# The first unit of a selective-scan block prepared by rows of its own

## The chip, the cores and the metric

The kernel runs on one core of a Trainium2 chip. The metric is the device time of one execution in microseconds. Five engines work side by side, each through its own list of instructions in order, and wait for one another by semaphores: TensorE (PE; matmuls into PSUM), VectorE (DVE), ScalarE (ACT), GpSimd (POOL), and SyncE (SP), whose queue issues DMA transfers. ScalarE can issue DMA transfers too. In the profile PEld is TensorE's load of weights, and SPq the issuing of DMAs on SyncE's queue.

## The reference, cut to what matters

x is 4 x 1024 x 128. A state-space block, a layer norm, a feed-forward block with weights and activations rounded to FP4 in blocks of 16, and another layer norm:

```python
u = silu(xp[:, :-2] * conv_w[0] + xp[:, 1:-1] * conv_w[1] + xp[:, 2:] * conv_w[2])
B, C = split(u @ W_bc + b_bc)                       # 16 states each
A = -exp(A_log)
dt = softplus((u @ W_dt + b_dt) @ W_dtp + b_dtp)
h[l] = exp(A * dt[l]) * h[l-1] + B[l] * x[l] * dt[l]   # per channel and state
y[l] = sum over the states of C[l] * h[l]
x = layernorm(x + y + x * Dcoeff)
hidden = silu(fp4(x) @ fp4(w_gate).T) * (fp4(x) @ fp4(w_up).T)
x = layernorm(x + fp4(hidden) @ fp4(w_down).T)
```

## The kernel before

The 4096 positions are cut into eight units of 512 (`UNITS`); two units make one sequence. Channels lie on the partitions. For the scan the 128 channels are cut into four quarters (`QUADS`) of 32, and each tile of 128 partitions holds 4 states x 32 channels, so there are 4 sets of states (`SETS`) x 4 quarters = 16 groups (`GROUPS`) in a unit.

The work is a pipeline in software. `run` calls on each engine `step(a, s, f, g, h, p)`: `s` is the unit that is scanned, `a` the next one, which is prepared meanwhile, and `f`, `g`, `h` are the three before, in the stages of the feed-forward block. Inside a step the engine goes through 16 slots k, one for each group; the table `AT` says in which slot a stage's instructions stand. The order of each engine's list is thus written by hand. The first call, with i = -1, has no `s`: it only prepares unit 0 (slot 0 transposes, slots 1 and 2 convolution, and so on) and does what the weights need before the first scan (`setup`, `setup_weights`).

The preparation of a unit, engine by engine:
- TensorE turns x (`ps_prep<-ident,x_tok`), ScalarE copies it to `x_feat`; TensorE convolves with three diagonal matrices (`tap_diag`, six matmul passes) and ScalarE takes tanh; VectorE makes `u_feat` (half of silu's argument times 1 + tanh).
- TensorE multiplies u by `wz` (W_dt W_dtp, itself made at the start), and ScalarE makes dt by Softplus, once into `dtx` and once into PSUM. Exp and tanh share a table of ScalarE, Softplus needs another, hence table loads around it. VectorE writes dt * x as the second half of `dtx`.
- SyncE's queue copies `dtx` to `dt_rep`, each of 4 quarters to 4 blocks of 32 partitions: 16 DMAs of 128 KB (`replicate`), counted per quarter by `dt_in`.
- TensorE makes C for each set (`ps_prep<-u_feat,wbc_rep`), four times two passes in the one bank `ps_prep`, and ScalarE takes each out to `c_rep`.

The scan of a unit: TensorE makes B for a set in `ps_b` (`spread_b`); VectorE multiplies it with the four quarters of `dt_rep` at once (`times_b`, the "product with B", 128x2048, into `db`); ScalarE makes the decays by Exp, one for each group (`decay`, `ps_decay`), two groups ahead; VectorE scans (`scan`, 16 for a unit, one for each group); GpSimd multiplies the states by C (`times_c`, two groups at a time); TensorE sums over the states in `ps_y` (`sum_states`). `times_b` for set m + 1 stands two groups ahead of its first scan, so the first one of the next unit comes before scan 14 of this one.

The feed-forward weights are rounded to FP4 by nine operations on VectorE (`quant_op` 0 to 8, into `qh_amax`, `qh_scale`, `qh_inv`, `qh_norm`, `qh_magic`, `hq`), turned by TensorE and taken by ScalarE to `gate_t`, `up_t` and `down_t`.

## Time and profile before

| | |
|---|---|
| time, median of 3 runs | 410.14 us (409.21 to 410.53) |
| the profiled execution's own time | 411.21 us |
| its span in the trace | 409.4 us |
| mean granted TensorE clock | 0.859 of full speed |
| busy: PE, DVE, ACT, POOL | 284.3 (69%), 333.6 (81%), 216.1 (53%), 281.5 (69%) us |
| DMA | 21.86 MB in 19246 packets, mean 53 GB/s |

Times in a view count from the span's start. A row of a timeline gives start, duration, engine, line, operation, output<-inputs, shapes, how many were merged, and in brackets the idle time before and what ended it. The granted clock is the share of TensorE's full 2.4 GHz that it was allowed; it has two levels, 0.5 and 1, and a number between is a mean over the stretch.

### The profile page before, as it was taken

How to read it: one execution, taken by the hardware profiler on the slowest of the kernel's cores; microseconds unless marked ns; L12 is line 12 of the kernel's file. 1: busy time of each engine (PE TensorE's matmuls, PEld its weight loads, DVE VectorE, ACT ScalarE, POOL GpSimd, SP SyncE). 2: the span in 40 equal slices, each digit the busy share in tenths (PEclk: the TensorE clock that was granted, in tenths of full speed). 3: DMA queues.
4: the chain of work that ended last, by engine and by line, in shares of the span. 5: the costliest groups of instructions: out<-in, count | busy, mean ns of one | idle time of the engine just before them, and what ended most of it. 6: DMA issues, size and time to landing. Idle time of an engine off the chain costs nothing.

```text
span 409.4 us, 3984 instructions
## 1 busy us (share of the span) xinstructions
PE 284.3 (69%) x1136; PEld 133.2 (33%) x1136; DVE 333.6 (81%) x374; ACT 216.1 (53%) x493; POOL 281.5 (69%) x168
## 2 busy tenths in 40 slices
PE   5478665677866784789397848778578765664783
PEld 2125111212412333334242325233333342234363
DVE  2828969799999999699978999699969998445880
ACT  2634663765575566465927482756546364133235
POOL 0003555568487997499929994799749995976652
PEclk9656698889969996999889996999699668598698
DMA  2470280081018005410261008100530000000001
GB/s 39 109 169 0 52 181 1 0 186 44 2 44 189 0 2 114 92 51 2 51 155 52 0 2 189 48 19 2 126 80 27 0 0 26 1 2 1 26 2 51
DMA packets 19246, 21.86 MB, mean 53 GB/s; under 512 B 6096, under 2 KB 15128, under 8 KB 19224
## 3 DMA queue, kind: packets, MB, share of 16 engines
q1 hardware_dynamic: 19224, 21.60, 23.2%
q8 instruction: 9, 0.15, 0.2%
q14 instruction: 13, 0.11, 0.1%
HBM read 2.72 MB, written 2.10 MB: 12 GB/s over the span
## 4 chain that ended last, share of the span: by engine, by line
PE 31%; POOL 27%; ACT 13%; issue 11%; DVE 11%; SPq 4%; DMA 2%; POOLq 0%; DVEq 0%; ACTq 0%
POOL product L654 8%; PE ps_f L1151 5%; PE ps_b L1111 5%; POOL qh_norm L675 4%; POOL qh_norm L670 4%; DVE states L862 4%; PE ps_prep L1089 4%; PE ps_y L1069 3%; DVE db L849 3%; PE ps_prep L1104 3%; PE ps_f L1149 2%; SPq L412 2%; POOL rstd L664 2%; POOL xq L694 2%; POOL qx_norm L675 2%
## 5 line engine op out<-in xcount | busy, mean ns | idle before, releaser
L654 POOL TENSOR_TENSOR product<-states,c_rep 128x1024 f32<-128x1024 f32 x64 | 150.7, 2360 | 60.3 <-DVE states L862 57.1
L450 ACT ACTIVATE ps_decay<-dt_rep,aneg 128x512 f32<-128x512 f32 x128 | 87.0, 693 | 38.2 <-DVE states L862 38.1
L862 DVE TENSOR_TENSOR_SCAN states<-ps_decay,states,db 128x512 f32<-128x512 f32 x64 | 79.9, 1263 | 14.1 <-POOL product L654 9.5
L849 DVE SCALAR_TENSOR_TENSOR db<-ps_b,bbc_rep,dt_rep 128x2048 f32<-128x2048 f32 x32 | 74.8, 2338 | 11.7 <-PE ps_b L1111 9.4
L862 DVE TENSOR_TENSOR_SCAN states<-ps_decay,db 128x512 f32<-128x512 f32 x64 | 76.3, 1207 | 8.6 <-issue 4.6
L1104 PE MATMUL ps_prep<-u_feat,wbc_rep 128*128 128x512 f32 x64 | 39.5, 701 | 22.5 <-ACT c_rep L516 19.4
L1111 PE MATMUL ps_b<-u_feat,wbc_rep 128*128 128x512 f32 x64 | 43.3, 765 | 16.4 <-DVE db L849 16.4
L1069 PE MATMUL ps_y<-product,gather 128*32 128x512 f32 x256 | 39.1, 687 | 6.0 <-POOL product L654 5.7
L1136 PE MATMUL ps_f<-gate_t,xq_t 128*128 128x352 f32 x64 | 30.1, 554 | 14.5 <-DVE hidden L916 8.9
L516 ACT ACTIVATE c_rep<-ps_prep,bbc_rep 128x512 f32<-128x512 f32 x32 | 22.1, 692 | 28.2 <-PE ps_prep L1104 28.2
L662 POOL TENSOR_TENSOR var_eps<-var,eps 128x4 f32<-128x4 f32 x16 | 3.5, 220 | 45.8 <-ACT hq_t L524 39.3
L554 ACT ACTIVATE gate_tanh<-ps_f 128x352 f32<-128x352 f32 x32 | 14.8, 464 | 36.8 <-PE ps_f L1136 36.8
L1089 PE MATMUL ps_prep<-x_feat,tap_diag 128*128 128x512 f32 x48 | 28.3, 711 | 5.4 <-ACT x_feat L491 4.6
L1149 PE MATMUL ps_f<-x,ident 128*128 128x128 f32 x44 | 12.3, 371 | 23.2 <-ACT hq_t L562 23.2
L1104 PEld LDWEIGHTS ps_prep<-u_feat,wbc_rep 128*128 128x128 f32 x64 | 10.4, 205 | 50.7 <-ACT c_rep L516 41.5
L524 ACT ACTIVATE hq_t<-ps_f 128x128 f32<-128x128 f32 x22 | 5.8, 278 | 39.9 <-PE ps_f L1151 39.9
L1144 PE MATMUL ps_f<-up_t,xq_t 128*128 128x352 f32 x64 | 26.3, 495 | 0.7 <-ACT y_out L575 0.7
L1111 PEld LDWEIGHTS ps_b<-u_feat,wbc_rep 128*128 128x128 f32 x64 | 13.8, 236 | 32.1 <-DVE db L849 21.4
L1151 PE MATMUL ps_f<-down_t,hq_t 128*128 128x128 f32 (+1 forms) x120 | 23.2, 348 | 0.0
L916 DVE SCALAR_TENSOR_TENSOR hidden<-gate_tanh,ps_f 128x352 f32<-128x352 f32 x32 | 16.1, 502 | 8.1 <-ACT gate_tanh L554 7.9
L1151 PEld LDWEIGHTS ps_f<-down_t,hq_t 128*128 128x128 f32 (+1 forms) x120 | 21.5, 262 | 0.0
L1136 PEld LDWEIGHTS ps_f<-gate_t,xq_t 128*128 128x128 f32 x64 | 10.4, 203 | 32.2 <-DVE hidden L916 21.9
(150 smaller groups left out, 505.1 us busy)
## 6 DMA issues: line engine op xcount, KB each, us to landing
dt_rep<-dtx SPq DMA_DIRECT2D x128, 128.0 KB, 2.4
x_tok<-in_L_attn_x SPq DMA_DIRECT2D x8, 256.0 KB, 3.0
out<-y_out SPq DMA_DIRECT2D x8, 256.0 KB, 2.3
hidden<-in_L_ffn_w_down SPq DMA_DIRECT2D x1, 176.0 KB, 2.5
x_feat<-in_L_attn_x SPq DMA_DIRECT2D x8, 0.5 KB, 2.7
hidden<-in_L_ffn_w_gate SPq DMA_DIRECT2D x1, 128.0 KB, 2.2
hidden<-in_L_ffn_w_up SPq DMA_DIRECT2D x1, 128.0 KB, 2.2
alog<-in_L_attn_A_log SPq DMA_DIRECT2D x4, 8.0 KB
```

Of the source, the lines that this page charges most:

```text
L450: nc.scalar.activation(ps_decay[BANK_OF[k]][:], dt_rep[p][:, c, 0, :], ACT.Exp, scale=aneg[:, c, m:m + 1]).then_inc(decay_done, 1)
L654: nc.gpsimd.tensor_tensor(product[:, j % PRODUCTS], states[p][:, first:first + 2, :], over(c_rep[p][:, j // SET_PAIRS, :], 2), ALU.mult).t ...
L675: order.mark(nc.gpsimd.tensor_tensor(b.norm[:, 0:width], b.norm[:, 0:width], b.magic[:, 0:width], ALU.subtract))
L849: nc.vector.scalar_tensor_tensor(out=db[m % DB][:], in0=over(ps_b[:], QUADS), scalar=bbc_rep[:, 0, m:m + 1], in1=dt_rep[p][:, :, 1, :], op ...
L862: nc.vector.tensor_tensor_scan(out=states[p][:, k % ring, :], data0=ps_decay[BANK_OF[k]][:], data1=db[k // QUADS % DB][:, k % QUADS, :], i ...
L1069: last = nc.tensor.matmul(ps_y[c * E:(c + 1) * E, :], gather[:], product[:, (m * SET_PAIRS + c // 2) % PRODUCTS, c % 2, :], start=False, s ...
L1089: last = nc.tensor.matmul(ps_prep[:], tap_diag[:, tap], x_feat[o][:, tap:tap + UNIT], start=(tap == 0), stop=(tap == 2))
L1104: nc.tensor.matmul(ps_prep[:], wbc_rep[:, 1, m], u_feat[o][:], start=True, stop=True)\
L1111: nc.tensor.matmul(ps_b[:], wbc_rep[:, 0, m], u_feat[o][:], start=True, stop=True).then_inc(b_mm, 1)
L1136: nc.tensor.matmul(ps_f1[:, 0:INNER], xq_t[:, i * 128:(i + 1) * 128], gate_t[:], start=True, stop=True).then_inc(gate_mm, 1)
L1144: nc.tensor.matmul(ps_f2[:, 0:INNER], xq_t[:, i * 128:(i + 1) * 128], up_t[:], start=True, stop=True).then_inc(up_mm, 1)
L1151: last = nc.tensor.matmul(bank[:, columns], hq_chunk(j, rows), down_t[0:rows, j, :], start=False, stop=(j == 2))
```

## The change

Unit 0 is no longer prepared by a call of `step`; each engine has a `head` of its own, and `run` starts with i = 0.

- **Convolution of unit 0 on VectorE**: three operations over 512 columns from `x_feat` with `half_taps`, into `conv_0` (room in `product`). `tap_diag` is made later, for unit 1 on. `wz` and `bz` are taken out by VectorE instead of ScalarE.
- **dt of unit 0** is made once, and VectorE makes dt * x from the copy in SBUF.
- **Copies from two queues**: SyncE copies quarters 0, 2 and 3 of unit 0, ScalarE's queue quarter 1; the four DMAs of `A_log` are issued by ScalarE at its very start instead of by SyncE.
- **C of unit 0 in `ps_y`**: `c_of_first` makes C for the first set in the head, and for the others in slots 0, 1 and 2 of the first step; the sums of that step wait until all are out (`head_c_done`).
- **First product with B in two halves** of two quarters (`half_times_b`); the second stands before scan 2. The second product with B of unit 0 moves to slot 4, and its matmul to slot 3 of TensorE.
- **Weights**: the last three operations of the FP4 rounding move to GpSimd; VectorE does the first six in the head. Turning them moves from slots 1 and 3 of the first step to 6 and 9, and taking them out from 2 and 4 to 7 and 10.

```diff
-    for i in range(-1, UNITS):
+    for i in range(UNITS):
...
+            replicate(Unit(0), 0, (0, 2, 3))
...
+            channels = a_log.rearrange("(c a e) k -> c a e k", c=QUADS, a=1)
+            for c in range(QUADS):
+                act.dma_start(alog[:, c, :], channels[c].broadcast_to([STATES, E, N])).then_inc(alog_in, 16)
...
+            def head(a):
+
+                act.wait_ge(prep_mm, 1)
+                nc.scalar.activation(x_feat[0][:, 1:UNIT + 1], ps_prep[:], ACT.Copy).then_inc(prep_evac, PREP_EVAC)
+                act.wait_ge(conv_done, 1)
+                nc.scalar.activation(tanh_c[:], conv_0, ACT.Tanh).then_inc(tanh_done, 1)
+                act.wait_ge(alog_in, 16 * QUADS)
+                nc.scalar.activation(aexp[:].rearrange("p c k -> p (c k)"), alog[:].rearrange("p c k -> p (c k)"),
+                                     ACT.Exp).then_inc(scan_ready, 1)
+                act.wait_ge(scan_ready, 1)
+                for n in range(STATES):
+                    rows = slice(n * E, (n + 1) * E)
+                    nc.scalar.activation(aneg[rows], aexp[rows].rearrange("p c (m n) -> p n c m", n=STATES)[:, n],
+                                         ACT.Copy, scale=-1.0).then_inc(scan_ready, 1)
+                act.wait_ge(z_ready, 2)
+                nc.scalar.activation(table_in[:, 1:2], bz[:], ACT.Softplus)
+                act.wait_ge(prep_mm, PREP_MM)
+                nc.scalar.activation(dtx[:, 0, :], ps_prep[:], ACT.Softplus, bias=bz[:]).then_inc(dt_out, 1)
+                act.wait_ge(dtx_done, 1)
+                act.wait_ge(dt_out, 1)
+                for n in range(STATES):
+                    act.dma_start(dt_rep[0][n * E:(n + 1) * E, 1], dtx[E:2 * E]).then_inc(dt_in[1], 16)
+                nc.scalar.activation(table_in[:, 2:3], bz[:], ACT.Exp)
+                act.wait_ge(scan_ready, 1 + STATES)
+                act.wait_ge(selectors, 1)
+                for k in range(AHEAD):
+                    decay(a, k, 0)
+                c_of_first(0)
+
+            def c_of_first(m):
+                act.wait_ge(head_c, m + 1)
+                nc.scalar.activation(c_rep[0][:, m, :], ps_y[:], ACT.Identity,
+                                     bias=bbc_rep[:, 1, m:m + 1]).then_inc(head_c_done, 1)
...
+                            if k < SETS - 1:
+                                c_of_first(k + 1)
...
-                if j == 0:
+                if j % SET_PAIRS == 0 and not s.beyond(1):
+                    pool.wait_ge(head_c_done, j // SET_PAIRS + 1)
...
+            nc.vector.tensor_scalar(half_taps[:], taps[:], 0.5, None, ALU.mult).then_inc(conv_order, 1)
...
+            dve.wait_ge(conv_order, 1)
+            dve.wait_ge(prep_evac, PREP_EVAC)
+            nc.vector.tensor_scalar(conv_0, x_feat[0][:, 1:UNIT + 1], half_taps[:, 1:2], None,
+                                    ALU.mult).then_inc(conv_order, 1)
+            dve.wait_ge(conv_order, 2)
+            nc.vector.scalar_tensor_tensor(out=conv_0, in0=x_feat[0][:, 0:UNIT], scalar=half_taps[:, 0:1], in1=conv_0,
+                                           op0=ALU.mult, op1=ALU.add).then_inc(conv_order, 1)
+            dve.wait_ge(conv_order, 3)
+            dve.wait_ge(halo_in[0], 16)
+            nc.vector.scalar_tensor_tensor(out=conv_0, in0=x_feat[0][:, 2:UNIT + 2], scalar=half_taps[:, 2:3], in1=conv_0,
+                                           op0=ALU.mult, op1=ALU.add).then_inc(conv_done, 1)
+            dve.wait_ge(z_weights, 1)
+            nc.vector.tensor_copy(wz[:], ps_f1[:, 0:D]).then_inc(z_ready, 1)
+            nc.vector.tensor_tensor(bz[:], ps_f1[:, D:D + 1], bdtp[:], ALU.add).then_inc(z_ready, 1)
+            dve.wait_ge(conv_done, 1)
+            dve.wait_ge(tanh_done, 1)
+            nc.vector.scalar_tensor_tensor(out=u_feat[0][:], in0=tanh_c[:], scalar=1.0, in1=conv_0,
+                                           op0=ALU.add, op1=ALU.mult).then_inc(u_done, 1)
...
+            def head():
+                dve.wait_ge(dt_out, 1)
+                nc.vector.tensor_tensor(dtx[:, 1, :], dtx[:, 0, :], x_feat[0][:, 1:UNIT + 1], ALU.mult).then_inc(dtx_done, 1)
+                for i in range(3):
+                    last = nc.vector.tensor_scalar(tap_diag[:, i], ident[:], half_taps[:, i:i + 1], None, ALU.mult)
+                setup.mark(last)
+                dve.wait_ge(w_in, 16 * 5)
+                for n in range(6):
                     setup.need()
                     last = quant_op(n, wraw, wquant, qh, WCOLS)
-                    if n < 8:
+                    if n < 5:
                         setup.mark(last)
                     else:
-                        last.then_inc(wq_ready, 1)
+                        last.then_inc(w_magic_done, 1)
...
+            def half_times_b(part):
+
+                cs = slice(2 * part, 2 * part + 2)
+                dve.wait_ge(b_mm, 1)
+                for c in range(QUADS)[cs]:
+                    dve.wait_ge(dt_in[c], 16 * STATES)
+                nc.vector.scalar_tensor_tensor(
+                    out=db[0][:, cs], in0=over(ps_b[:], 2), scalar=bbc_rep[:, 0, 0:1], in1=dt_rep[0][:, cs, 1, :],
+                    op0=ALU.add, op1=ALU.mult).then_inc(db_done if part else db_half, 1)
...
+                if k < 2 and not s.beyond(1):
+                    dve.wait_ge(db_half, 1)
+                else:
+                    dve.wait_ge(db_done, s.at(SETS, k // QUADS + 1))
                 nc.vector.tensor_tensor_scan(
...
                     at = later(s, a, k, LEAD, p) if (k + LEAD) % QUADS == 0 else None
-                    if at:
+                    if k == 2 and not s.beyond(1):
+                        half_times_b(1)
+                    elif at:
                         times_b(at[0], at[1] // QUADS, at[2])
+                    if k == 4 and not s.beyond(1):
+                        times_b(s, 1, p)
                     if k == AT["dve u"] and a is not None:
                         u_of(a, 1 - p)
-                    if a is not None and not a.beyond(1):
-                        setup_weights(k)
...
+            head()
+            half_times_b(0)
...
+            def head(a):
+                pe.wait_ge(x_in[0], 16)
+                for i in range(TILES):
+                    last = nc.tensor.transpose(ps_prep[:, i * 128:(i + 1) * 128], x_tok[0][:, i, :], ident[:])
+                last.then_inc(prep_mm, 1)
+                pe.wait_ge(z_in, 16 * 4)
+                nc.tensor.matmul(ps_f1[:, 0:D], wdt_t, wdtp, start=True, stop=True)
+                nc.tensor.matmul(ps_f1[:, D:D + 1], wdtp, bdt[:], start=True, stop=True).then_inc(z_weights, 1)
+                pe.wait_ge(prep_evac, PREP_EVAC)
+                pe.wait_ge(z_ready, 2)
+                pe.wait_ge(u_done, 1)
+                nc.tensor.matmul(ps_prep[:], wz[:], u_feat[0][:], start=True, stop=True).then_inc(prep_mm, PREP_MM - 1)
+                pe.wait_ge(selectors, 1)
+                spread_b(a, 0, 0)
+                c_of_first(0)
+
+            def c_of_first(m):
+                if m:
+                    pe.wait_ge(head_c_done, m)
+                nc.tensor.matmul(ps_y[:], wbc_rep[:, 1, m], u_feat[0][:], start=True, stop=True).then_inc(head_c, 1)
...
+                elif m == 0:
+                    pe.wait_ge(head_c_done, SETS)
...
+                    if not s.beyond(1) and k < SETS - 1:
+                        c_of_first(k + 1)
+                    if not s.beyond(1) and k == 3:
+                        spread_b(s, 1, p)
```

The order on TensorE in the first step shows two of these moves at once. `ps_y<-u_feat,wbc_rep` and, before, `ps_prep<-u_feat,wbc_rep` are matmuls of C; `ps_b` is B; `ps_prep<-x_feat,tap_diag` is the convolution of unit 1. Before, from the product with wz of unit 0 to that of unit 1:

```order
L1097 MATMUL ps_prep<-u_feat,wz 128x512
L1104 MATMUL ps_prep<-u_feat,wbc_rep 128x512 x4
L1111 MATMUL ps_b<-u_feat,wbc_rep 128x512 x2
L1080 MATMUL ps_prep<-ident,x_tok 128x128 x4
L1046 MATMUL ps_f<-ident,hq 128x128 x2
...
L1089 MATMUL ps_prep<-x_feat,tap_diag 128x512 x3
L1111 MATMUL ps_b<-u_feat,wbc_rep 128x512
```

And with the change, the same stretch, behind the product with wz of unit 0:

```order
L1193 MATMUL ps_b<-u_feat,wbc_rep 128x512
L1118 MATMUL ps_y<-u_feat,wbc_rep 128x512 x2
L1164 MATMUL ps_prep<-ident,x_tok 128x128 x4
L1118 MATMUL ps_y<-u_feat,wbc_rep 128x512
L1173 MATMUL ps_prep<-x_feat,tap_diag 128x512
L1118 MATMUL ps_y<-u_feat,wbc_rep 128x512
L1173 MATMUL ps_prep<-x_feat,tap_diag 128x512 x2
L1193 MATMUL ps_b<-u_feat,wbc_rep 128x512 x2
L1179 MATMUL ps_prep<-u_feat,wz 128x512
```

The C matmuls moved in between the transposes and the convolution of unit 1, the weights left, and the second matmul of B moved from ahead of unit 1's transposes to behind its convolution.

On ScalarE, before, from the first C of unit 0 to the tanh of unit 1, with what each waits for:

```order
L516 ACTIVATE c_rep<-ps_prep,bbc_rep 128x512 [waits prep_mm,selectors,scan_ready]
L516 ACTIVATE c_rep<-ps_prep,bbc_rep 128x512 [waits prep_mm] x3
L450 ACTIVATE ps_decay<-dt_rep,aneg 128x512 [waits dt_in0]
L450 ACTIVATE ps_decay<-dt_rep,aneg 128x512 [waits dt_in1]
L450 ACTIVATE ps_decay<-dt_rep,aneg 128x512 [waits dt_in2]
L450 ACTIVATE ps_decay<-dt_rep,aneg 128x512 [waits scan_done,dt_in3]
L491 ACTIVATE x_feat<-ps_prep 128x512 [waits prep_mm]
```

With the change:

```order
L460 ACTIVATE ps_decay<-dt_rep,aneg 128x512 [waits dt_in0,selectors,scan_ready]
L460 ACTIVATE ps_decay<-dt_rep,aneg 128x512 [waits dt_in1]
L494 ACTIVATE c_rep<-ps_y,bbc_rep 128x512 [waits head_c]
L460 ACTIVATE ps_decay<-dt_rep,aneg 128x512 [waits dt_in2]
L494 ACTIVATE c_rep<-ps_y,bbc_rep 128x512 [waits head_c]
L460 ACTIVATE ps_decay<-dt_rep,aneg 128x512 [waits scan_done,dt_in3]
L494 ACTIVATE c_rep<-ps_y,bbc_rep 128x512 [waits head_c]
L516 ACTIVATE x_feat<-ps_prep 128x512 [waits prep_mm]
```

C used to be taken out ahead of all decays; now each C stands behind a decay that waits for copies, and three of the four ahead of unit 1's x_feat.

## Rows read from the trace of the kernel before

**Rows 1.** The page: the chain that ended last, shares by engine.
```profile
PE 31%; POOL 27%; ACT 13%; issue 11%; DVE 11%; SPq 4%; DMA 2%; POOLq 0%; DVEq 0%; ACTq 0%
```

**Rows 2.** That chain in order of time, 178 to 223 us: start, duration, what.
```profile
178.74 2.87 POOL qh_norm L670
...
222.94 2.87 POOL qh_norm L670
```

**Rows 3.** The same chain, 16 to 60 us.
```profile
16.83 0.61 DVE dtx L874
...
29.95 2.36 DVE db L849
...
46.64 0.68 DVE dtx L874
...
56.93 3.69 DMA dt_rep<-dtx
```

**Rows 4.** Timeline of the head, 4 to 19 us.
```profile
4.45 0.36 SPq L386 DMA_DIRECT2D bdtp<-in_L_attn_b_dtp  x1
...
4.80 0.60 ACT L491 ACTIVATE x_feat<-ps_prep 128x512 f32<-128x512 f32 x1 [2.57 <-PE ps_prep L1080]
...
5.50 5.25 PE L1089 MATMUL ps_prep<-x_feat,tap_diag 128*128 128x512 f32 x6 [0.73 <-issue]
...
6.27 2.42 SPq L394 DMA_DIRECT2D alog<-in_L_attn_A_log  x4
...
10.63 0.29 DVE L793 TENSOR_SCALAR skip_diag<-ident,dskip 128x128 f32<-128x128 f32 x1
...
11.63 0.60 ACT L497 ACTIVATE tanh_c<-ps_prep 128x512 f32<-128x512 f32 x1
...
12.26 0.69 DVE L881 SCALAR_TENSOR_TENSOR u_feat<-tanh_c,ps_prep 128x512 f32<-128x512 f32 x1 [1.34 <-ACT tanh_c L497]
...
13.30 1.32 DVE L806 TENSOR_REDUCE qh_amax<-hidden 128x70 f32<-128x1120 f32 x1 [0.34 <-DMA hidden<-in_L_ffn_w_down]
...
14.81 0.67 ACT L507 ACTIVATE dtx<-ps_prep,bz 128x512 f32<-128x512 f32 x1
...
18.12 0.45 DVE L823 TENSOR_SCALAR qh_magic<-qh_magic 128x1120 bf16<-128x1120 bf16 x1
```

**Rows 5.** DMA issues of 17 to 30 us, and two stretches (last columns: clock, DMA share, GB/s).
```profile
dt_rep<-dtx SPq DMA_DIRECT2D x16, 128.0 KB, 2.4
...
12.00:13.00 1.00, 0.00 (x0) 0.00 (x0) 0.69 (x1) 0.92 (x5) 0.00 (x0) 1.00 0.87 256
20.00:25.00 5.00, 3.80 (x4) 1.01 (x4) 2.62 (x2) 1.06 (x2) 0.00 (x0) 0.50 0.94 209
```

**Rows 6.** Timeline of the first step, 26 to 61 us.
```profile
26.13 2.07 PE L1104 MATMUL ps_prep<-u_feat,wbc_rep 128*128 128x512 f32 x2 [0.78 <-ACT c_rep L516]
...
28.24 0.69 ACT L516 ACTIVATE c_rep<-ps_prep,bbc_rep 128x512 f32<-128x512 f32 x1 [2.16 <-PE ps_prep L1104]
...
32.35 2.08 PE L1111 MATMUL ps_b<-u_feat,wbc_rep 128*128 128x512 f32 x2 [2.44 <-DVE db L849]
...
36.25 3.50 PE L1089 MATMUL ps_prep<-x_feat,tap_diag 128*128 128x512 f32 x6
...
36.90 2.33 DVE L862 TENSOR_TENSOR_SCAN states<-ps_decay,db 128x512 f32<-128x512 f32 x2
...
40.41 0.69 DVE L881 SCALAR_TENSOR_TENSOR u_feat<-tanh_c,ps_prep 128x512 f32<-128x512 f32 x1 [1.19 <-ACT tanh_c L497]
...
42.98 1.28 ACT L507 ACT_TABLE_LOAD   x1
...
60.84 2.35 DVE L849 SCALAR_TENSOR_TENSOR db<-ps_b,bbc_rep,dt_rep 128x2048 f32<-128x2048 f32 x1 [2.06 <-DMA dt_rep<-dtx]
```

**Rows 7.** Stretches: length, busy PE, PEld, DVE, ACT, POOL, clock, DMA share, GB/s.
```profile
35.00:40.00 5.00, 5.00 (x15) 2.92 (x14) 4.23 (x3) 2.82 (x6) 2.95 (x2) 0.73 0.00 0
...
50.00:60.00 10.00, 7.63 (x26) 1.78 (x18) 7.60 (x6) 5.65 (x10) 5.58 (x3) 0.93 0.89 203
```

More of the change, by code:

```diff
@@ L629, in tail @@
                 normalised(f, p, tail_tile)
+            head(Unit(0))
             run(step, tail)
@@ L775, in _ @@
             dve.wait_ge(taps_in, 16)
-            for i in range(3):
-                last = nc.vector.tensor_scalar(tap_diag[:, i], ident[:], taps[:, i:i + 1], 0.5, ALU.mult, ALU.mult)
-            last.then_inc(taps_ready, 1)
+            nc.vector.tensor_scalar(half_taps[:], taps[:], 0.5, None, ALU.mult).then_inc(conv_order, 1)
             nc.vector.tensor_scalar(center[:], ident[:], 1.0 / D, None, ALU.subtract)
@@ L1251, in tail @@
                 project_tile(TILES - 1)
+            head(Unit(0))
             run(step, tail)
```

96 lines of the change are left out of this document (35 added, 61 removed).

## The prediction

> **What bounds the kernel now.** I read the chain of waits first, for the whole span. Its shares [rows 1] name no single engine; TensorE and GpSimd lead with 31% and 27%. Read in order of time it falls into two parts. From about 130 us on, it repeats: the same GpSimd rounding add comes back after 44.20 us, 222.94 less 178.74 [rows 2], and so does what lies between. The change touches nothing there. So the question is when that train sets off.
>
> The front of the chain answers it [rows 3]. Unit 0's dtx is written at 17.44 us (16.83 + 0.61); its first product with B starts at 29.95; unit 1's dtx is written at 47.32 (46.64 + 0.68); its copies are issued one after another until the last landing at 60.62; unit 1's first product with B starts at 60.84 [rows 6]. Every later step hangs on that last moment. Whatever brings unit 1's dtx forward brings the end forward by as much, as long as its copies remain the last thing that the product waits for: VectorE stood idle for the 2.06 us before it, and the row names the copies as what it waited for [rows 6].
>
> Then the timelines: of the head [rows 4], of the copies [rows 5], and of the first step [rows 6]; and granted clock by stretch [rows 7].
>
> **The head, part by part.** Before, TensorE's convolution takes 5.50 to 10.75 and tanh ends at 12.23 [rows 4]. After it, VectorE convolves as soon as x_feat is there (5.40). The trace has no such operation from SBUF alone: one pass over 512 columns costs 0.69 with a PSUM operand (u_feat) [rows 4]; skip_diag over 128 columns, which a quarter of the columns must not exceed, costs 0.29. So the first of the three operations costs 0.3 to 0.7 and the other two 0.69 each; with waits between, I take 2.0 (1.7 to 2.2): 7.4. Tanh 0.60 gives 8.05. Beside it run wz and bz: the last of their vectors is issued by 4.81 and, at the 2.4 us of the copies [rows 5], in by 7.2; two small matmuls, a copy and an add after it make 8.2. From the end of tanh to the end of the Softplus, before took 3.25 (12.23 to 15.48), all on ScalarE: A, a table load, Softplus. That stays: 11.3. But the product with wz is now on a TensorE that did little, and at the lower clock a pair takes 2.08 [rows 6]; u is ready at 8.9, so it ends at 11.0 and the Softplus at 11.7. The second Softplus (into PSUM) is gone, dtx takes 0.68 more: 12.4, against 17.44. The selectors, which before were ready at 10.92, now come behind u but are still there before the product with wz ends. **The head wins 5.0.**
>
> What ScalarE has new in front: four issues of A's rows (before 2.42 in all on the sync queue [rows 4]), then the table load of 1.28 and a dummy of 0.2. From 0.7 that ends at 4.6, just ahead of the 4.80 at which x_feat could start. I count 0; uncovered, it costs one for one. VectorE has the weight quantisation behind dtx: 13.30 to 18.57 before, less dtx and plus tap_diag, so from 12.4 to about 18. That is hidden by the copies, of which the first two quarters are not in before 19. GpSimd takes the last three steps of the weights, about 2.87 x 1120/1408 = 2.3 each [rows 2], 18 to 25; before, it had nothing to do until the first product with C. The weights themselves are needed only in the next step.
>
> **Copies from two queues.** 16 copies of 128 KB land 2.4 us after issue, and during them the DMA engines are 94% busy at 209 GB/s [rows 5]. At that rate they are the limit, not the queue: 2.1 MB take 10.0 us from whatever queue. But the weight load moved 256 GB/s at 87% [rows 5]; had the copies that rate for their busy share, they would take 7.6. I take 10.0, the row of the same transfer. Then quarters 0 and 1, which now share the engines, are both in at 19.2 (12.4 + 2.4 + 7 x 0.63), and quarter 3 at about 24.3. The Trainium skill, "DMA: Bandwidth & Descriptors", section "Issuing engines are not separate DMA queues", says that transfers started by several engines run on the same 16 DMA engines and interleave, and only the time of issue is saved. By it the second queue is worth nothing here; by the 256 GB/s it is worth 2.4.
>
> **The first step: where the gain shrinks.** Half of the product with B (1.2) and scans 0 and 1 run at 19.2 to 22.8, the other half and scans 2 and 3 from 24.3 to 28. Before, the same work, with a second product more, ended at 39.2 [rows 6]. That looks like 11 us, but it isn't what unit 1 waits for. Two things are new in the order of TensorE. The matmuls of C, which before were done by 28.2 [rows 6], now stand between unit 1's transposes and convolution, each behind an evacuation by ScalarE, and ScalarE has decays in between. And the second matmul of B, which before came right behind the first product (32.35), now stands behind the whole convolution of unit 1. The second product with B on VectorE waits for it, and behind that product, on the same engine, stand unit 1's u, scans 4 to 6 and unit 1's dtx.
>
> Followed step by step, with 2.08 for a pair of passes at the lower clock and 0.69 for an evacuation or a decay [rows 6]: decays 0 and 1 to 20.3, C0 out at 20.95; C1 21.0 to 23.05, out at 23.8; C2 to 25.9 (decay 3 fits between), out at 26.65; x_feat 0.60: 27.2. From 27.25 TensorE is dense with 10 passes: convolution 6, C3 2, B 2. A pass takes 0.875 at the lower clock (5.25/6) [rows 4] and about 0.45 at the higher one. Before, a dense stretch that began at 34.22 got the higher clock at 37.5 (the mean of 0.73 for 35 to 40 is 0.50 for half of it [rows 7]), while the convolution at 5.50 ran all 5.25 us at the lower pace [rows 4]. So the rise comes 3.3 to 5.3 after the start; at 4.3 it leaves 5 passes fast: B is ready at 33.9 (all slow 36.2, all fast 31.8).
>
> From there to unit 1's dtx: from u on, before took 6.91 (40.41 to 47.32 [rows 3, 6]), the second product stands ahead with 2.3: **43.1**. ScalarE's line in parallel (scan 4, decay 7, table load 1.28, two Softplus) takes 7.5 and is hidden. Against 47.32 that is **4.2 us earlier**. The copies of unit 1 follow at the same 13.5. Behind dtx ScalarE has the weights' evacuations (some 1.5) among C and decays; about 0.6 of it finds no gap, and the 2 us of VectorE's idle time cover it; without that cover the step would start 0.6 later.
>
> **Sum.** 409.4 - 4.2 = 405.2 of span. The profiled execution took 411.21, 1.07 over the median of 410.14; against the median, 410.14 - 4.2 = **405.9 us**.
>
> **Rivals.**
> 1. The clock rises late: B and convolution all slow, B ready at 36.2, dtx 45.4, gain 1.9: 408.2. For it: in 20 to 25 us TensorE was busy 3.80 of 5 us and stayed at 0.50 [rows 5]. The Trainium skill, "TensorE: Matmul & The Clock Gate", section "What's actually happening", says that the moment isn't tied to the kernel's start, so it may vary from run to run.
> 2. More gain, by an early rise (C1 and C2 with their gaps count as dense: C2 1.0 faster, then all fast: 30.9, gain 7.2, 402.9) or by the second queue moving 256 GB/s (quarters 0 and 1 some 1.2 earlier: gain 5.4, 404.7). Against the first stands the same 0.50.
> 3. The shift is given back: unit 1's copies are no longer last in the first step, because VectorE's scans 12 and 13 wait for decays queued behind the C evacuations. Cover is 2.06; if ScalarE's weight work and slow C pairs (0.96 each, four of them) exceed it by all 3.8 + 0.6 - 2.1 = 2.3, 408.2 is left, and with half the clock's loss 409.2: no difference.
> 4. Slower: the clock stays at its lower level from 27 us through the whole first step, C pairs included. Gain 1.9, less 2.3 as in 3, less 1.0 or so in the next step's gather passes: 411.5. It decides once the level stays low past about 50 us. Against it: before, the stretch from 50 to 60 us had 0.93 of full clock [rows 7].
> 5. The head does not shorten: ScalarE's issues take twice as long beside the sync queue's, 4.8 instead of 2.4; then x_feat is 2.3 late, the rest of the chain with it, gain 1.9: 408.2.
>
> **Chances.** Forecast 0.52 (its own range 404.4 to 407.4, from the rise at 3.3 to 5.3 us, 2.2 or 1.7 for the convolution, and 0.7 of landing times). Rival 1 0.13, rival 2 0.13, rival 3 0.09, rival 4 0.05, rival 5 0.08. The range 402.8 to 409.2 leaves out rival 4, and tails of rivals 2 and 3. A measurement of this kernel can tell about 0.3%, 1.2 us, from nothing. Faster by more: forecast, 2, most of 1 and 5, half of 3: 0.88. Within: 0.08. Slower: 0.04.
>
> **What would show it.** Right if: dtx of unit 0 is written at 12 to 13; the copies still move about 209 GB/s; VectorE waits several us for ps_b ahead of the second product, until about 34; unit 1's dtx near 43; its product with B 13.5 behind; the GpSimd add still comes back after 44.2. Wrong if B's second matmul is early (then more gain), if unit 1's product waits for VectorE's own scans instead of copies, or if the first x_feat starts after 5.5.

## The result

The changed kernel took 403.5 us (median of 4 runs, 402.41 to 404.13) beside 410.33 us (median of 4, 409.21 to 411.11) for the kernel before: ratio 0.9833, 95% interval 0.98 to 0.9865. Forecast were 405.9 us and 402.8 to 409.2. It came out faster and inside the stated range, by 2.4 us more than forecast; 403.5 lies outside the forecast's own 404.4 to 407.4, and only the room left for the rivals holds it. The profiled execution took 403.82 us with a span of 402.0, against 411.21 and 409.4 before, so the spans differ by 7.4 us.

The page of the changed kernel, its first lines and the shares of its chain, which stand beside [rows 1]:

```profile
span 402.0 us, 3984 instructions
...
PE 276.5 (69%) x1130; PEld 131.6 (33%) x1130; DVE 332.3 (83%) x378; ACT 214.8 (53%) x490; POOL 288.3 (72%) x171
...
PE 31%; POOL 27%; ACT 13%; issue 11%; DVE 10%; SPq 4%; DMA 3%; POOLq 0%; DVEq 0%; ACTq 0%
```

The shares hardly moved; a chain that starts earlier looks the same. GpSimd has the weights' last three operations more than before; an experiment below puts their price. TensorE has six matmuls and six weight loads fewer, the convolution of unit 0. The prediction gave these twelve instructions no part in the rest of the kernel; they have one.

**The head**, timeline of the changed kernel, beside [rows 4]:

```profile
0.74 2.97 ACTq L450 DMA_DIRECT2D alog<-in_L_attn_A_log  x4
...
2.75 1.97 SPq L394 DMA_DIRECT2D states<-in_L_attn_W_dtp  x1
...
5.11 0.55 SPq L394 DMA_DIRECT2D bdtp<-in_L_attn_b_dtp  x1
5.15 0.58 ACT L466 ACTIVATE x_feat<-ps_prep 128x512 f32<-128x512 f32 x1
...
7.14 0.75 DVE L823 SCALAR_TENSOR_TENSOR product<-x_feat,half_taps,product 128x512 f32<-128x512 f32 x1
...
7.97 0.79 PE L1105 MATMUL ps_f<-states 8*128 8x128 f32 x2 [3.01 <-DMA bdtp<-in_L_attn_b_dtp]
...
9.29 0.68 DVE L830 SCALAR_TENSOR_TENSOR u_feat<-tanh_c,product 128x512 f32<-128x512 f32 x1
...
10.11 2.05 PE L1110 MATMUL ps_prep<-u_feat,wz 128*128 128x512 f32 x2 [1.14 <-DVE u_feat L830]
...
12.20 0.69 ACT L480 ACTIVATE dtx<-ps_prep,bz 128x512 f32<-128x512 f32 x1 [0.97 <-PE ps_prep L1110]
...
12.92 0.69 DVE L883 TENSOR_TENSOR dtx<-dtx,x_feat 128x512 f32<-128x512 f32 x1 [0.56 <-ACT dtx L480]
```

VectorE's convolution runs from 5.83 to 7.89: 2.06, as summed. But TensorE waits for the last small vector (b_dtp) until 7.97, and `wz`, which stands ahead of u on VectorE, holds u back to 9.29. Unit 0's dtx is there at 13.61 and not at 12.4.

**The first step**, timeline of the changed kernel, beside [rows 6]:

```profile
21.11 1.28 DVE L902 SCALAR_TENSOR_TENSOR db<-ps_b,bbc_rep,dt_rep 128x1024 f32<-128x1024 f32 x1 [2.01 <-DMA dt_rep<-dtx]
...
22.37 0.67 ACT L494 ACTIVATE c_rep<-ps_y,bbc_rep 128x512 f32<-128x512 f32 x1
...
25.51 1.28 DVE L902 SCALAR_TENSOR_TENSOR db<-ps_b,bbc_rep,dt_rep 128x1024 f32<-128x1024 f32 x1 [0.67 <-DMA dt_rep<-dtx]
...
25.94 1.57 PE L1118 MATMUL ps_y<-u_feat,wbc_rep 128*128 128x512 f32 x2
...
28.13 0.59 ACT L516 ACTIVATE x_feat<-ps_prep 128x512 f32<-128x512 f32 x1
...
28.77 1.13 PE L1173 MATMUL ps_prep<-x_feat,tap_diag 128*128 128x512 f32 x2 [1.27 <-ACT x_feat L516]
...
33.37 2.35 DVE L913 SCALAR_TENSOR_TENSOR db<-ps_b,bbc_rep,dt_rep 128x2048 f32<-128x2048 f32 x1 [4.13 <-PE ps_b L1193]
...
41.85 0.67 DVE L940 TENSOR_TENSOR dtx<-ps_prep,x_feat 128x512 f32<-128x512 f32 x1
...
54.76 2.35 DVE L913 SCALAR_TENSOR_TENSOR db<-ps_b,bbc_rep,dt_rep 128x2048 f32<-128x2048 f32 x1 [2.04 <-DMA dt_rep<-dtx]
```

And the windows of the same stretch (length, busy PE, PEld, DVE, ACT, POOL, clock, DMA share, GB/s):

```profile
15.00:20.00 5.00, 1.20 (x2) 0.00 (x0) 3.94 (x6) 1.49 (x2) 0.74 (x1) 1.00 1.01 200
20.00:25.00 5.00, 1.91 (x3) 0.77 (x4) 3.62 (x3) 2.60 (x4) 4.84 (x3) 0.50 0.87 213
...
26.00:27.00 1.00, 1.00 (x3) 0.44 (x2) 0.90 (x2) 0.47 (x1) 1.00 (x2) 0.57 0.00 0
27.00:28.00 1.00, 0.51 (x2) 0.00 (x0) 1.00 (x1) 0.46 (x1) 1.00 (x1) 1.00 0.00 0
```

What to see: VectorE waits 4.13 us for `ps_b`, the named stall, up to 33.37 (forecast 33.9). It got there by another road. Everything in front is 0.9 to 1.9 later than forecast, because of the head, and TensorE's clock is at its higher level from 26.9 us (0.57 in 26 to 27, then 1.00), during C's third matmul, so that the convolution's pair takes 1.13 and not 2.08. For the head the clock's column can't be used: it reads 1.00 for 10 to 12 us too, where a pair takes 2.05 (the row at 10.11), the pace of the lower level.

### The profile page after: what moved, and what is told of

It reads as the page before. It is cut to its first block, busy times and chain, and to the rows that moved or that the text cites. A ratio compares the mean times of both kernels' runs of the same rounds, so it can differ in the third digit from the quotient of the medians.

```text
span 402.0 us, 3984 instructions
## 1 busy us (share of the span) xinstructions
PE 276.5 (69%) x1130; PEld 131.6 (33%) x1130; DVE 332.3 (83%) x378; ACT 214.8 (53%) x490; POOL 288.3 (72%) x171
## 4 chain that ended last, share of the span: by engine, by line
PE 31%; POOL 27%; ACT 13%; issue 11%; DVE 10%; SPq 4%; DMA 3%; POOLq 0%; DVEq 0%; ACTq 0%
POOL product L677 8%; PE ps_f L1233 5%; PE ps_b L1193 5%; POOL qh_norm L698 4%; POOL qh_norm L693 4%; DVE states L929 3%; PE ps_y L1152 3%; DVE db L913 3%; SPq L417 3%; PE ps_prep L1173 3%; PE ps_f L1231 2%; PE ps_y L1149 2%; POOL xq L717 2%; POOL rstd L687 2%; POOL qx_norm L698 2%
## 5 line engine op out<-in xcount | busy, mean ns | idle before, releaser
L460 ACT ACTIVATE ps_decay<-dt_rep,aneg 128x512 f32<-128x512 f32 x128 | 87.1, 693 | 39.6 <-DVE states L929 36.6
L913 DVE SCALAR_TENSOR_TENSOR db<-ps_b,bbc_rep,dt_rep 128x2048 f32<-128x2048 f32 x31 | 72.5, 2338 | 8.7 <-PE ps_b L1193 6.4
L1186 PE MATMUL ps_prep<-u_feat,wbc_rep 128*128 128x512 f32 x56 | 31.4, 643 | 16.4 <-ACT c_rep L536 16.3
L685 POOL TENSOR_TENSOR var_eps<-var,eps 128x4 f32<-128x4 f32 x16 | 3.6, 223 | 44.4 <-ACT hq_t L544 39.6
L536 ACT ACTIVATE c_rep<-ps_prep,bbc_rep 128x512 f32<-128x512 f32 x28 | 19.4, 693 | 17.9 <-PE ps_prep L1186 17.8
L1173 PE MATMUL ps_prep<-x_feat,tap_diag 128*128 128x512 f32 x42 | 21.7, 624 | 4.2 <-ACT x_feat L516 4.2
L1186 PEld LDWEIGHTS ps_prep<-u_feat,wbc_rep 128*128 128x128 f32 x56 | 8.6, 195 | 37.3 <-ACT c_rep L536 33.2
```

Source lines behind the costliest of these rows:

```text
L460: nc.scalar.activation(ps_decay[BANK_OF[k]][:], dt_rep[p][:, c, 0, :], ACT.Exp, scale=aneg[:, c, m:m + 1]).then_inc(decay_done, 1)
L913: nc.vector.scalar_tensor_tensor(out=db[m % DB][:], in0=over(ps_b[:], QUADS), scalar=bbc_rep[:, 0, m:m + 1], in1=dt_rep[p][:, :, 1, :], op ...
L1173: last = nc.tensor.matmul(ps_prep[:], tap_diag[:, tap], x_feat[o][:, tap:tap + UNIT], start=(tap == 0), stop=(tap == 2))
L1186: nc.tensor.matmul(ps_prep[:], wbc_rep[:, 1, m], u_feat[o][:], start=True, stop=True)\
```

## Where 7.4 us came from

The table below takes its times from the rows named so far. "Copies" runs from unit 1's dtx to its first product with B, "second step" from that product to unit 2's u. These rows of the changed kernel end at unit 2's u:

```profile
62.15 1.13 PE L1173 MATMUL ps_prep<-x_feat,tap_diag 128*128 128x512 f32 x2 [0.69 <-ACT x_feat L516]
...
66.90 0.69 DVE L947 SCALAR_TENSOR_TENSOR u_feat<-tanh_c,ps_prep 128x512 f32<-128x512 f32 x1 [0.59 <-ACT tanh_c L522]
```

The same two rows of the kernel before:

```profile
68.30 1.98 PE L1089 MATMUL ps_prep<-x_feat,tap_diag 128*128 128x512 f32 x2 [2.36 <-ACT x_feat L491]
...
74.64 0.69 DVE L881 SCALAR_TENSOR_TENSOR u_feat<-tanh_c,ps_prep 128x512 f32<-128x512 f32 x1 [2.21 <-ACT tanh_c L497]
```

| | before | after | gain |
|---|---|---|---|
| unit 1's dtx written | 47.32 | 42.52 | 4.8 |
| its copies, to the product with B | 13.52 | 12.24 | 1.3 |
| second step, to unit 2's u | 13.80 | 12.14 | 1.7 |
| unit 2's u to the end of the span | 334.8 | 335.1 | -0.3 |

Forecast was the first line alone, at 4.2. The third goes with TensorE's clock: in 65 to 70 us before it was granted 0.84 on the mean, and from the first pair of unit 2's convolution to its u it took 6.34 and not 4.75. Why the clock fell there was not found. The second line needed a cause. The DMA view of 54 to 62 us before (the product starts at 60.84):

```profile
q1 hardware_dynamic: 1038, 1.24, 67.8%
q8 instruction: 1, 0.02, 0.9%
...
x_tok<-in_L_attn_x SPq DMA_DIRECT2D x1, 256.0 KB, 3.8
```

After, 49 to 56 us (the product starts at 54.76):

```profile
q1 hardware_dynamic: 1056, 1.28, 80.3%
...
x_tok<-in_L_attn_x SPq DMA_DIRECT2D x1, 256.0 KB, 3.1
```

Before, a load of 16 KB of instructions (queue q8) fell among the copies; it begins at 58.3 us. After, it begins at 58.4, when the product has already started. This is a correlation in two traces; the experiments below test it.

## The experiments

The kernel before was timed beside each of three groups and took 410.71 us (17 runs; the first four experiments below), 411.01 (17; the next four) and 410.81 (15; the last four), so groups differ by some 0.3 us. The runs of one kernel scatter more than that: where the intervals of two kernels overlap, the difference of their medians is not told from nothing, and only the profile speaks. "Profile" means the one profiled execution. In brackets stand the ratio to the kernel before and its 95% interval. Diffs are against the changed kernel.

**The changed kernel again**, to compare with.

> The changed kernel once more, as the control of its call. If the 6.8 us are real and do not hang on a lucky moment of the clock, it is 6.5 to 7.2 us under the kernel before again, unit 1's dtx is written at 42.3 to 42.8 us and its first product with B starts 12.2 us later (54.8). If the extra over the forecast 4.2 was chance (a lucky clock in the second step, a late last copy in the trace of before), it is 4 to 6 us under, and the 12.2 becomes 13.5.

403.84 us (ratio 0.9855, interval 0.9811 to 0.99), span again 402.0. Its dtx of unit 0 came at 13.0, not 13.6: the last vector landed 2.56 after issue instead of 2.82 and was issued 0.4 earlier. So some 0.6 of the head varies between executions of one kernel. Its copies took 12.18 and its second step 12.14, as in the first profile.

**The first product with B whole**

```diff
-            half_times_b(0)
+            times_b(Unit(0), 0, 0)
...
-                if k < 2 and not s.beyond(1):
-                    dve.wait_ge(db_half, 1)
-                else:
-                    dve.wait_ge(db_done, s.at(SETS, k // QUADS + 1))
+                dve.wait_ge(db_done, s.at(SETS, k // QUADS + 1))
```

> The first product with B of unit 0 in one piece again, over all four quarters. Theory: it must wait for the last quarter (25.5), scan 0 starts at 27.9 instead of 22.5; decay 3 waits for scan 0 (it needs its bank) and stands on ScalarE ahead of the taking out of C2 and of unit 1's x_feat, so unit 1's x_feat, convolution, B and dtx come about 3.2 us later: 406.7 us. Rival: VectorE sat idle for 4.1 us ahead of the second product anyway, so the halves are worth nothing: 403.5.

408.79 us (0.9949, 0.9926 to 0.9972): 5.0 slower. The profile shows 3.3 of it, unit 1's dtx at 45.7 and not 42.2. The order gives 2.0 of these 3.5: the fourth decay waits for the first scan, and behind it on ScalarE stand C's third evacuation and unit 1's x_feat, at 29.8 and not 27.8. Most of the rest is the clock, which the expectation left out: the convolution's first pair fell on the lower level (granted 0.53 in 30 to 33 us), where the repeated changed kernel's took 1.12.

```profile
30.45 2.08 PE L1168 MATMUL ps_prep<-x_feat,tap_diag 128*128 128x512 f32 x2 [3.31 <-ACT x_feat L516]
```

The other 1.7 of the medians has no place in that profile, which is of one of the fastest of the twelve runs (407.09; 406.89 to 410.15).

**All copies from the sync queue**

```diff
-            replicate(Unit(0), 0, (0, 2, 3))
+            replicate(Unit(0), 0)
...
-                for n in range(STATES):
-                    act.dma_start(dt_rep[0][n * E:(n + 1) * E, 1], dtx[E:2 * E]).then_inc(dt_in[1], 16)
```

> All sixteen copies of unit 0 from the sync queue, in the order of quarters; ScalarE issues none of them. Theory (the engines are the limit, 200 to 210 GB/s from whatever queue): quarter 1 is in at 21.1 as before, quarter 3 at 25.5, and the time stays within 0.5 us of 403.5. Rival (the second queue moves more): both come 1 us or more later, and the time rises by 1 to 2.4 us, to 404.5 or more.

402.92 us (0.9814, 0.979 to 0.9838): not slower, and the profile is 1.7 shorter. The expected price of 1.0 to 2.4 us, had the second queue moved more, is not there. Timeline of this kernel:

```profile
20.03 1.28 DVE L898 SCALAR_TENSOR_TENSOR db<-ps_b,bbc_rep,dt_rep 128x1024 f32<-128x1024 f32 x1 [1.66 <-DMA dt_rep<-dtx]
20.55 0.67 ACT L490 ACTIVATE c_rep<-ps_y,bbc_rep 128x512 f32<-128x512 f32 x1
...
25.01 1.29 DVE L898 SCALAR_TENSOR_TENSOR db<-ps_b,bbc_rep,dt_rep 128x1024 f32<-128x1024 f32 x1 [1.25 <-DMA dt_rep<-dtx]
```

Both halves start within 0.4 us of the repeated changed kernel's (20.4 and 24.8). With one queue quarter 0 is in earlier: no other quarter moves beside it, and the first decay starts at 17.34 and not 20.46. C's first evacuation (20.55, not 21.7) and what follows come earlier too. So the second queue shows no gain. The Trainium skill, "DMA: Bandwidth & Descriptors", section "Issuing engines are not separate DMA queues", says that DMAs started by different engines run on the same 16 DMA engines and interleave. This run agrees: with the copies on one queue or two the second half starts at 25.0 or 24.8.

**B's second matmul ahead of unit 1's convolution**

```diff
-                    if not s.beyond(1) and k == 3:
+                    if not s.beyond(1) and k == 1:
                         spread_b(s, 1, p)
```

> The second matmul of B of unit 0 moves from slot 3 to slot 1 on TensorE, ahead of unit 1's convolution; nothing else. Theory (its place behind the convolution is what kept VectorE waiting 4.1 us): the second product with B starts at about 29.3 instead of 33.4, the convolution is 0.5 to 1 later, and unit 1's dtx comes 1.2 to 2 us earlier, held then by ScalarE's line of tanh, decay 7, table load and Softplus: 401.5 to 402.3 us. Rival (the convolution and tanh hold unit 1's u anyway, and B is only late by the same): no gain, or 0.5 us lost.

402.63 us (0.9796, 0.9769 to 0.9823), 1.2 under the changed kernel; the profile is 3.5 shorter (398.5). The product with B starts at 28.49 and no longer waits for TensorE, and unit 1's dtx comes at 39.6. So B's place did cost 2.6 in the trace. The 1.2 of the medians is not clear of noise, since the intervals overlap, and the profiled run is the fastest of the six.

**Convolution of unit 0 back on TensorE** (the rest of the change kept; `tap_diag` made ahead of it on VectorE)

```diff
-            nc.vector.tensor_scalar(conv_0, x_feat[0][:, 1:UNIT + 1], half_taps[:, 1:2], None,
-                                    ALU.mult).then_inc(conv_order, 1)
...
+                for tap in range(3):
+                    last = nc.tensor.matmul(ps_prep[:], tap_diag[:, tap], x_feat[0][:, tap:tap + UNIT],
+                                            start=(tap == 0), stop=(tap == 2))
+                last.then_inc(conv_done, 1)
```

> The convolution of unit 0 back on TensorE (six passes), with its diagonal matrices made ahead; all else as changed. Theory: six passes at 0.875 take 5.3 us from 5.8 against 2.06 on VectorE, less the faster product with wz behind it (1.34 instead of 2.05, as before) and less the wait for wz, which held u until 9.3: dtx of unit 0 is written at 15.5 to 16.2 instead of 13.6, and all that follows is 2 to 2.6 us later: 405.5 to 406.1 us. Rival (the head's gain comes from the rest, since wz and the Softplus line take until 12 anyway): within 0.7 us of 403.5.

410.52 us (0.9988, 0.9956 to 1.0019): the whole gain is gone, and expected was about a third of it, so the expectation missed. In the profile (span 409.6): dtx of unit 0 2.6 later (15.6); unit 1's convolution at the lower clock (its first pair 2.07), so dtx of unit 1 4.3 later (46.5); copies 13.76, with the instruction load among them; the second step 14.51. The expected 2 to 2.6 is right for the head. The rest of the 7.6 by which the spans differ comes from three terms that the expectation did not have: the clock in unit 1's convolution, the load among the copies, and the second step.

**The four issues for A_log back on the sync queue, behind the vectors**, and A made after the Softplus

```diff
-            for c in range(QUADS):
-                act.dma_start(alog[:, c, :], channels[c].broadcast_to([STATES, E, N])).then_inc(alog_in, 16)
...
+            for c in range(QUADS):
+                sp.dma_start(alog[:, c, :], channels[c].broadcast_to([STATES, E, N])).then_inc(alog_in, 16)
```

> The four transfers of A_log back to the sync queue, behind those of the small vectors; A is computed behind the Softplus, after ScalarE's table is back. Theory (these four transfers at the very start are why my head was 1.2 us too early: they held the sync queue's issues and the landing that wz waits for): x_feat starts at 4.8 instead of 5.15, the small matmuls for wz start at 6.9 instead of 8.0, and dtx of unit 0 is written at 12.5 to 12.9 instead of 13.6; decays wait 0.5 more for nothing. Total 402.5 to 403.0 us. Rival (the landing is late for another reason, the thousand 4-byte pieces of W_dt on the same queue): 403.5, with the small matmuls still at 7.9.

403.22 us (0.9819, 0.9777 to 0.9861), 0.6 under the repeated changed kernel; that is less than the timing tells apart. Profile 400.4. Two things were moved here, the four issues and the making of A; the earlier rows below stand ahead of A in either kernel, so they are the issues' doing. Timeline of this kernel:

```profile
2.72 1.26 SPq L394 DMA_DIRECT2D states<-in_L_attn_W_dtp  x1
...
4.66 0.60 ACT L466 ACTIVATE x_feat<-ps_prep 128x512 f32<-128x512 f32 x1 [2.43 <-PE ps_prep L1102]
...
6.53 0.79 PE L1105 MATMUL ps_f<-states 8*128 8x128 f32 x2 [1.98 <-DMA bdtp<-in_L_attn_b_dtp]
```

The issue of W_dtp takes 1.26 again and not 1.97, x_feat is 0.5 earlier and the small matmuls 1.4 earlier than in the changed kernel's first profile (0.8 earlier than in its second). dtx of unit 0 comes at 12.5, the time once forecast.

**Five matmuls more ahead of the first step**, to bring the clock up (their result is not used)

```diff
                 c_of_first(0)
+                for _ in range(5):
+                    nc.tensor.matmul(ps_f2[:], ident[:], u_feat[0][:], start=True, stop=True)
```

> Five more matmuls of 512 columns (ten passes) on TensorE in the head, behind the first C, into a bank that nobody reads before it is overwritten; they fill the gap from 16.2 to 23.1. Theory (C1 and C2 of unit 0 run at the lower clock, 2.07 for a pair, on the line that ends in unit 1's dtx): the higher clock is granted when C1 starts, C1 and C2 take 1.1 each, and unit 1's dtx is 1.4 us earlier: 402.1 us. Rival (the clock falls again before it matters, or C3 and the convolution lose what C1 and C2 win): within 0.5 us of 403.5.

404.16 us (0.9841, 0.9792 to 0.989): no gain where 1.4 us was hoped for. The profile is of the slowest of the six runs (408.92, the others 401.80 to 407.21; without it the median is 403.64), so it tells where that run's time went and nothing of the rest. There C1 and C2 took 2.07 each all the same, the convolution's first pair took 2.07 too, dtx of unit 1 came at 44.0, and the instruction load, at 54.4, fell among the copies (13.61). The times alone say that this extra work did not bring the gain that was expected of it.

**C's first evacuation ahead of the first decays on ScalarE**

```diff
+                c_of_first(0)
                 for k in range(AHEAD):
                     decay(a, k, 0)
-                c_of_first(0)
```

> On ScalarE, C of the first set is taken out ahead of decays 0 and 1, not behind them. It has been in its bank since 16.2, while ScalarE waits for copies until 21.1. Theory (each C waits for the one before to be taken out, and the first waits for copies for no reason): C1 is ready at about 21, is taken out behind decay 2 at 24.0, and unit 1's x_feat comes 1.2 us earlier: 402.3 us. Rival (decay 3 waits for the last quarter of the copies or for scan 0 and holds the line as before): within 0.5 us of 403.5.

404.95 us (0.9873, 0.9836 to 0.991), 1.1 over, within the overlap of the intervals; the hoped 1.2 of gain is not there. Timeline of this kernel:

```profile
26.82 0.59 ACT L516 ACTIVATE x_feat<-ps_prep 128x512 f32<-128x512 f32 x1
...
27.46 2.07 PE L1173 MATMUL ps_prep<-x_feat,tap_diag 128*128 128x512 f32 x2 [1.27 <-ACT x_feat L516]
...
34.01 2.35 DVE L913 SCALAR_TENSOR_TENSOR db<-ps_b,bbc_rep,dt_rep 128x2048 f32<-128x2048 f32 x1 [5.29 <-PE ps_b L1193]
```

x_feat is 1.0 earlier than the repeated one's 27.8, as hoped, but the convolution's first pair now runs at the lower clock, which rises only at 31.4 (granted 0.50 in 30 to 31, 0.79 in 31 to 32) and not at 26.9, and B is 1.0 later. In this profile the clock took back twice what the order gave. The work is the same; only its place differs.

**Twelve TensorE instructions more, early or late.** The two are one experiment: three matmuls of one column (six passes and six weight loads; results unused), in the head or in unit 1's step of the feed-forward block, behind the load in question.

```diff
+                for _ in range(3):
+                    nc.tensor.matmul(ps_f2[:, 0:1], ident[:], u_feat[0][:, 0:1], start=True, stop=True)
```

> Three matmuls of one column each behind the first C in the head, into a bank nobody reads before it is overwritten: twelve instructions of TensorE (six weight loads, six passes), under 1 us of work in a gap of 7 us. They give back the twelve instructions by which the change shortened TensorE's list ahead of the first step. Theory I (the 16 KB instruction load on the DMA rings comes when TensorE's list reaches a certain length; in the changed kernel it falls 3.5 us behind the copies of unit 1, before the change and with twelve more it falls among them, holds the last one, and TensorE's longer pause loses the clock): the copies take 13.5 us or more again from dtx to product instead of 12.2, unit 1's product with B starts 1.3 us later though dtx is written at the same time, u of unit 2 is 3 to 4 us later, and the time is 406.5 to 408. Rival C (the two levels are a matter of the clock's moments alone): 403.5 within 0.7, copies at 12.2.

> The same three small matmuls, but in slot 3 of the third step, behind the instruction load in question: the control of the kernel with twelve early ones. Theory I: nothing in the first two steps changes, copies at 12.2, time 403.5 within 0.7. Rival (any twelve instructions more cost the time, or shift later loads): as slow as the kernel with them early.

Early: 407.99 us (0.9916, 0.9881 to 0.9951). Late: 403.75 (0.9832, 0.9795 to 0.9868). The DMA view of 49 to 56 us, twelve early:

```profile
q1 hardware_dynamic: 1030, 1.21, 75.0%
q8 instruction: 1, 0.02, 0.8%
...
x_tok<-in_L_attn_x SPq DMA_DIRECT2D x1, 256.0 KB, 3.7
```

The same view, twelve late:

```profile
q1 hardware_dynamic: 1011, 1.16, 73.1%
...
x_tok<-in_L_attn_x SPq DMA_DIRECT2D x1, 256.0 KB, 3.0
```

Three one-column matmuls move the load from 57.9 to 52.6 us, into the copies, and these take 13.04 instead of 12.18. That shows the cause of the second line of the table, and 0.9 of its 1.3: an instruction load among the copies. The other 0.4 may hang on where among them it falls, which was not tested. The rest of the theory missed: unit 2's u was to be 3 to 4 us later and is 1.2 later (the second step takes 12.13 beside 12.14), so that the median lies in its 406.5 to 408 by luck. Of the 4.2 that the two medians differ by, 3.2 stand in the last unit (from its u to the end 130.7 and 127.5). Windows of the kernel with twelve early (clock behind POOL's column):

```profile
380.00:385.00 5.00, 3.46 (x8) 1.62 (x7) 4.96 (x17) 0.93 (x2) 1.68 (x2) 0.77 0.00 0
...
390.00:395.00 5.00, 5.00 (x34) 5.00 (x34) 1.58 (x4) 0.00 (x0) 0.86 (x2) 0.71 0.01 3
```

With twelve late:

```profile
380.00:385.00 5.00, 2.54 (x12) 1.55 (x12) 4.93 (x14) 1.29 (x3) 2.64 (x4) 1.00 0.00 0
...
390.00:395.00 5.00, 5.00 (x47) 4.96 (x45) 0.59 (x2) 3.60 (x18) 1.99 (x3) 1.00 0.01 3
```

From 390 us TensorE is busy all the time, and the clock drops there in one and not in the other: the matmuls done in the same 5 us are 34 and 47. The early kernel's ten runs fall in two groups, three of 404.3 to 404.7 and seven of 407.1 to 408.8, and the profiled one (407.82) is of the larger. The mean granted clock of a whole run is 0.866 to 0.870 in all seven and 0.877 or 0.878 in the three (0.877 to 0.882 in the late kernel's six), so the upper group goes with a lower clock; that it falls in the tail is seen in one profile. The three lie 0.5 to 1.0 over the late kernel's median, about what the copies cost. The changed kernel has such a run too (408.27, clock 0.870), so the twelve instructions do not alone make the upper group.

**The weights' rounding on VectorE alone** (its last three operations back from GpSimd)

```diff
-                for n in range(6):
+                for n in range(9):
```

> The last three steps of the weights' rounding go back from GpSimd to VectorE, which does all nine in the head. Theory: VectorE is busy until about 23.1 (4.0 us more) instead of 19.1, so the first half product starts at 23.1 instead of 20.4 and scan 0 at 24.5; decay 3, which stands ahead of C2 and unit 1's x_feat, starts at 25.7, about when it does now, so unit 1's dtx moves by 0 to 0.5 us: 403.5 to 404.0 us. Rival (the 2.7 us of the first half product pass on to unit 1): 405 or more.

404.22 us (0.9852, 0.9805 to 0.99), 0.4 over the changed kernel, less than can be told. The first half of the product starts at 22.5 instead of 20.4, but unit 1's dtx only 0.2 later: slack that the wait for `ps_b` covers. One more thing stands in this profile: its copies take 12.2, with the instruction load behind them, and its second step takes 13.57 and not 12.14, with the granted clock low from 58.5 to 65.3. The loss in the second step thus comes without a load among the copies, as with twelve early such a load came without the loss. The two are separate.

**One queue, B early and A_log on the sync queue together**

> The three edits that brought unit 1's dtx forward, together: all copies from the sync queue, the second matmul of B ahead of unit 1's convolution, A_log's transfers on the sync queue. Theory: dtx of unit 0 at 12.5, C and x_feat 1.3 earlier, B 2.6 earlier; unit 1's dtx at 37.5 to 39 instead of 42.2, copies at 12.2, so 399.0 to 400.5 us, unless the instruction load then falls among the copies. Rival (the clock takes it back: TensorE pauses longer): 401.5 to 402.5.

399.61 us (0.974, 0.9704 to 0.9777): the best version here, 11.2 under the kernel before and 4.2 under the changed one, with no overlap of the intervals, and inside the expected 399.0 to 400.5. Its timeline:

```profile
28.59 2.33 DVE L909 SCALAR_TENSOR_TENSOR db<-ps_b,bbc_rep,dt_rep 128x2048 f32<-128x2048 f32 x1
...
31.83 0.69 DVE L943 SCALAR_TENSOR_TENSOR u_feat<-tanh_c,ps_prep 128x512 f32<-128x512 f32 x1 [0.92 <-ACT tanh_c L518]
...
38.06 0.67 DVE L936 TENSOR_TENSOR dtx<-ps_prep,x_feat 128x512 f32<-128x512 f32 x1
...
50.88 2.35 DVE L909 SCALAR_TENSOR_TENSOR db<-ps_b,bbc_rep,dt_rep 128x2048 f32<-128x2048 f32 x1 [0.51 <-DMA dt_rep<-dtx]
```

Unit 1's dtx is at 38.7, 3.8 ahead of the changed kernel's, and its span (397.8) 4.2 shorter. The wait for the copies has shrunk to 0.51, from 2.04: by this row, more than 0.5 us won in front of them would meet VectorE's own scans.

## The prediction, step by step

- **The head wins 5.0**: 3.8 and 4.4 in the two profiles (dtx at 13.6 and 13.0). The convolution was right to 0.1. The terms that failed are the landing of wz's vectors, "issued by 4.81" and "in by 7.2" (5.66 and 7.93 in the first profile), and "I count 0" for ScalarE's issues. These ended at 3.71 with the table load to 5.02 behind, so x_feat started at 5.15; and the sync queue's own issue beside them slowed. Moving them off (dtx at 12.5) shows the price: 0.5 to 1.1. This is rival 5 at a fifth to a half of its size.
- **Copies at 10.0 us from either queue**: right. From the first issue near 13.7 the second half could start at 25.51, at 200 to 213 GB/s; the experiment with one queue confirms it. What was said of quarters 0 and 1, both in at 19.2, came at 21.11; 1.2 of that is the head's, 0.7 was not foreseen.
- **B's second matmul behind the convolution**: right in place, stall and time (33.37 against 33.9). But two errors cancel, which is luck: the head was 1.2 late, and the clock rose at 26.9 instead of 31.5, which is near rival 2's early rise. The experiment with B ahead of the convolution takes the stall away and 2.6 with it. The forecast took the clock's rise from how long TensorE had been dense before; with C taken out first, the same work in another order, the rise came at 31.4. (The row of before, 0.73 for 35 to 40, puts its rise at 37.7, not 37.5; that changes nothing here.)
- **Unit 1's dtx at 43.1, 4.2 earlier**: 42.5, 4.8 earlier.
- **"The copies of unit 1 follow at the same 13.5"**: wrong, 12.24. This is one of two steps that failed, with 1.3 of the 3.2 by which the span fell short of the forecast 405.2. The copies' length depended on an instruction load that the removal of twelve TensorE instructions put behind them. In 14 profiles (the kernel before, the changed one and the 12 of the experiments) the load lies among the copies in the four that have twelve or more TensorE instructions more ahead of it; these take 13.0 to 13.8, the ten others 12.15 to 12.24. The pair with twelve early and twelve late shows the cause, for 0.9 us.
- **The rest repeats**: from about 140 us on 44.1 to 44.4 us per step, as before, and from unit 2's u to the end the same within 0.3. But the second step was not the same: 1.7 shorter, with the clock at its higher level in unit 2's convolution. This is the other step that failed, and the larger; the sum had no term for it. The runs show that it does not follow from the copies (the experiments with the weights' rounding and with twelve early), and of the kernel before there is one profile; its cause stays open. So 3.0 of the gain in the trace came from terms that the prediction put at nothing.
- **Weights to GpSimd at nothing**: right (0.4, not told apart from 0).

In all 4.8 + 1.3 + 1.7 - 0.3 = 7.5, beside 7.4 of the spans (rounding) and 6.8 of the medians. What stays open: the whole product loses 5.0 in the median where its profile shows 3.3; the time of most experiments varies by 1 to 4 us between runs of one kernel, and one profile each shows only one of these; and what sets the moment at which the clock changes was not found. The Trainium skill, "TensorE: Matmul & The Clock Gate", section "What's actually happening", says that this moment is not tied to the kernel's start. No run here tests that: the rise ahead of unit 1's convolution, or in it, comes at 26.9 us in both profiles of the changed kernel, at 31.4 with C first and at 37.7 before [rows 7], but these kernels differ in their work too.

## What to carry to other kernels

Ask of a wait not only who ends it but what stands behind it in order: here two half products were worth 5.0 us in the medians and 3.3 in the trace, because a decay, C and the next unit's x_feat were queued behind the first scan, and moving one matmul ahead of six others 2.6 in the trace. Issue a first transfer so that its earliest part is alone on the DMA engines; a second issuing queue gave nothing that can be told, with the engines busy 87 to 101% of the time. And expect an edit in front to shift everything behind it against two things that no dependency shows, the instruction loads and the clock: compare a stretch that should be the same (here the copies, 13.5 and 12.2) before calling a gain understood.
